# A vision block with routed experts on one core: where the expert numbers are read, when two weight packs are fetched, and where a norm stands

## What is computed

```python
def _L0_ffn_ref(x, router_w, w1, b1, w2, b2, gamma, beta):
    logits = xf @ router_w
    gate_vals, idx = jax.lax.top_k(logits, K)        # K = 2 of 8 experts
    gates = jax.nn.softmax(gate_vals, axis=-1)
    out = jnp.zeros_like(xf)
    for e in range(E):
        h = jax.nn.relu(xf @ w1[e] + b1[e]) @ w2[e] + b2[e]
        y = _layernorm(xf + h, gamma[e], beta[e])
        w = jnp.sum(jnp.where(idx == e, gates, 0.0), axis=-1)
        out = out + w[:, None] * y
    return out.reshape(B, S, D)
...
h = h + _L0_attn_ref(_layernorm(h, axis=-1), ...)
h = h + _L0_ffn_ref(_layernorm(h, axis=-1), ...)
```

## Time and profile before

| | |
|---|---|
| median of 3 runs | 144.37 us (144.24 to 144.65) |
| profiled execution, its own time | 144.59 us |
| its span, first to last instruction | 142.8 us |
| PE busy | 130.9 us (92% of the span) |
| VectorE busy | 104.4 us (73%) |
| ScalarE busy | 72.9 us (51%) |
| POOL busy | 57.3 us (40%) |
| mean granted TensorE clock | 0.940 |

### The profile page before, as it was taken

The page is one execution under the profiler, slowest core; times in us unless marked ns, Lnnn a source line. Parts: engine busy times, 40 slices in busy tenths (PEclk is TensorE's granted clock), DMA queues, the critical chain, the costliest instruction groups (busy, mean ns, idle before and its releaser), DMA issues. The chain is left out here.

```text
span 142.8 us, 3886 instructions
## 1 busy us (share of the span) xinstructions
PE 130.9 (92%) x1210; PEld 114.2 (80%) x1210; DVE 104.4 (73%) x417; ACT 72.9 (51%) x214; POOL 57.3 (40%) x96
## 2 busy tenths in 40 slices
PE   7999899999999999889993899999999999999960
PEld 7944898788759898668930879999999999999950
DVE  1479999979988667778664029887878789988580
ACT  5534315834476531139900006887878977896000
POOL 8900000000000046775778131377677767680010
PEclk9999999999999999999555569999999999999999
DMA  4999399999993019611115477598999751015405
GB/s 117 263 457 418 156 387 414 404 339 274 278 270 113 5 17 333 255 50 56 45 56 101 179 166 221 133 317 277 243 334 311 239 163 41 21 33 167 175 0 149
DMA packets 16423, 28.47 MB, mean 199 GB/s; under 512 B 1793, under 2 KB 9878, under 8 KB 16276
## 3 DMA queue, kind: packets, MB, share of 16 engines
q1 hardware_dynamic: 13700, 25.43, 55.3%
q0 software_dynamic: 1152, 2.07, 4.3%
q10 hardware_dynamic: 1552, 0.73, 2.2%
HBM read 19.55 MB, written 12.09 MB: 222 GB/s over the span
## 5 line engine op out<-in xcount | busy, mean ns | idle before, releaser
L1457 PE MATMUL ps<-w_all,hid 128*128 (+1 forms) x184 | 24.7, 278 | 0.3 <-issue 0.2
L1457 PEld LDWEIGHTS ps<-w_all,hid 128*128 128x128 f32 x184 | 22.4, 192 | 1.0 <-issue 0.8
L503 POOL DMA_INDIRECT back<-kTm,xg x16 | 15.9, 997 | 12.2 <-ACT kTm L693 6.1
L684 ACT ACTIVATE hid<-ps,D 128x128 f32<-128x128 f32 x48 | 13.5, 362 | 13.7 <-PE ps L1438 13.7
L1150 PE MATMUL ps<-zeros 128*128 128x128 f32 x112 | 17.8, 312 | 2.9 <-POOL SQ L490 2.9
L1150 PEld LDWEIGHTS ps<-zeros 128*128 128x128 f32 x112 | 16.1, 222 | 3.9 <-POOL SQ L490 3.4
L471 POOL TENSOR_TENSOR ex<-e_base,dlt 128x5 f32<-128x5 f32 x1 | 1.2, 1207 | 44.8 <-DVE dlt L935 44.8
L464 POOL DMA_INDIRECT rows<-x2k,row_at x16 | 16.1, 1007 | 6.9 <-issue 5.0
L1054 DVE COPY xgT<-ps 128x128 f32<-128x128 f32 x23 | 6.7, 290 | 10.1 <-PE ps L1430 8.4
L1438 PE MATMUL ps<-xgT,D 128*128 128x128 f32 x96 | 12.8, 276 | 0.0
L684 ACT ACTIVATE hid<-ps,last_parts 128x128 f32<-128x128 f32 x44 | 12.4, 364 | 0.0
(11 more groups left out here) (236 smaller groups left out, 278.4 us busy)
## 6 DMA issues: line engine op xcount, KB each, us to landing
rows<-blank SPq DMA_DIRECT2D x8, 589.5 KB, 6.7
D<-pack SPq DMA_DIRECT2D x12, 386.0 KB, 5.2
last_parts<-pack SPq DMA_DIRECT2D x11, 386.0 KB, 4.8
pack<-w1b SPq DMA_DIRECT2D x1, 2064.0 KB, 15.6
w_all<-w SPq DMA_DIRECT2D x1, 2048.0 KB, 12.2
back<-zeros SPq DMA_DIRECT2D x1, 1152.0 KB, 9.0
xg<-rows SPq DMA_DIRECT2D x16, 65.5 KB, 3.0
xT_oT<-patches SPq DMA_DIRECT2D x2, 512.0 KB, 5.9
```

The costliest lines, as they stand in the source:

```text
L503: nc.gpsimd.indirect_dma_start(back, bass.IndirectOffsetOnAxis(ap=xg[j][:, P:P + 1].bitcast(U32), axis=0), z[j], None, bounds_check=P * K ...
L684: nc.scalar.activation(hid[j % 2][:, f, :], ps[:, 2 + 2 * (j % 2) + f // 2, f % 2 * P:(f % 2 + 1) * P], ACT.Relu, bias=packed[j % NW][:, H ...
L1457: last = mm(ps[:, 6 + j % 2, 0:P], hid[j % 2][:, f, :], w2_all[:, bass.ds(expert_j, 1), f, :].rearrange("p a n -> p (a n)"), start=(f == 0 ...
```

## The change

Four edits:

1. PE reads all 18 expert numbers in front of the loop, right behind the matmuls on beta (line 1424) and ahead of the warming matmuls; `second_product` then takes them from a list. PE's wait for `slots_done` moves there too.
2. SP holds the packs of slots 5 and 6 back: it first reads its expert and tile numbers and issues the four local row loads, then these two packs.
3. VectorE's `normalise_group(3)`, the norm of tiles 7 and 8, moves from ahead of `rank_tables(1)` to behind `places(1)`. On PE `rank(1)` moves ahead of `turn_norm2(2)` with it.
4. On ACT `twice(1)`, a copy, moves behind the loading of the table for Exp and the exponential of part 1.

```diff
@@ sync
+            expert_at(0)
-            for j in range(FIXED, FIRST_ROWS):
-                load_pack(j)
             tile_at(FIRST_ROWS - FIXED)
             for j in range(SENT, SLOTS):
                 tile_at(j - FIXED)
             for j in range(SENT, SLOTS):
                 load_rows(sp, j, tile_at(j - FIXED))
+            for j in range(FIXED, FIRST_ROWS):
+                load_pack(j)
             sp.wait_ge(xg_loaded[row_sem(2)], 16)
@@ scalar
-            twice(1)
             nc.scalar.activation(table_scrap[:, 3:4], zeros[:, 0:1], ACT.Exp)
             exp_gates(1)
+            twice(1)
             copy_norm2(2)
@@ vector
             choose(1)
-            normalise_group(3)
             rank_tables(1)
             gates(1)
             places(1)
+            normalise_group(3)
             choose(2)
@@ tensor
             keep_warm(KEEP_WARM[9], 2)
+            rank(1)
             turn_norm2(2)
-            rank(1)
             route(2)
@@ tensor, the loop
-            w2_experts = {}
+            pe.wait_ge(slots_done, 2)
+            w2_experts = list(range(FIXED))
+            for s in range(0, FREE, 4):
+                w2_experts += list(four_values(mybir.EngineType.PE, expert_of, s, EXPERTS - 1))
 
             def second_product(j):
-                if j < FIXED:
-                    expert_j = j
-                else:
-                    if j not in w2_experts:
-                        for i, x in enumerate(four_values(mybir.EngineType.PE, expert_of, j - FIXED, EXPERTS - 1)):
-                            w2_experts[FIXED + (j - FIXED) // 4 * 4 + i] = x
-                    expert_j = w2_experts[j]
+                expert_j = w2_experts[j]
...
             pe.wait_ge(token_cols_set, 1)
             keep_warm(REWARM, 7)
-            pe.wait_ge(slots_done, 2)
```

## The result

The changed kernel takes **147.55 us** (median of 4 runs, 147.34 to 147.98) where the kernel before, beside it on the same chip, takes 144.48 (144.24 to 144.65, 4 runs). The ratio is 1.0217, with a 95% interval of 1.0188 to 1.0246. It is slower by 3.1 us. The profiled execution of it took 147.34 us, with a span of 145.5 and a mean granted clock of 0.928 (0.940 before).

A forecast was written before the change was run, and what follows sets the result against it. PE was taken to bound the end. Late warming +4.9, clock -0.2 and gaps -1.23 make +3.5 us on the profiled 144.59, so 148.1, or 147.8 as median (0.22 lower); own range 146.3 to 148.9, outer ends 145.5 and 149.3.

The forecast's parts named there:

- slots_done: Slot numbers ahead of PE's reads: ready at 76.3, not 73.80, from 1.7 us of later norm and 0.8 of half clock.
- Five reads, 7.8 us: PE's queue ahead of the warming: five reads of expert numbers take 7.8 us together, bounds 6.5 and 8.5.
- The rival in which reads are cheap in front: Ahead of the warming: all five reads fit into the idle 2.88 us, leaving only the saving, 143.3 us; chance 0.07.
- The warming +4.9: Ahead of PE's expert loop: the warming starts when the reads end, at 84.1 and not 79.20, +4.9 us.
- The clock, worth -0.2: During the warming: full clock returns after about 5.0 us, 0.4 less at half clock, -0.2 us; bounds -0.9 and +0.9.
- The gaps, -1.23: In PE's expert loop: array time lost at the first four reads (0.47, 0.21, 0.24, 0.31) goes away, -1.23 us.
- The end is PE's: Last stretch, 128 to 138: PE is busy throughout, so moving its loop's start or a slot moves the end equally.
- The rows down at 80.4, worth nothing: Row dispatch before the loop: rows down at 80.4, not 81.6, a 1.2 us gain alone, counted as nothing behind late warming.
- rival 3: Ahead of the reads: the norm's move is absorbed, slots_done stays at 73.8, reads end at 81.6, 145.5 us; chance 0.12.
- the sum said +3.5: Whole kernel: +4.9 - 0.2 - 1.23 = +3.5 us against the profiled execution's 144.59, that is 148.1.

The follow-up runs named there:

- b1: The kernel before with only the first three of PE's five reads in front of the warming, the last two in the loop; ratio 0.9984.
- b0: The changed kernel as it is, run again on another chip; ratio 1.0212 to the kernel before.
- c3: The changed kernel as it is, run again on a further chip beside its two halves; ratio 1.0164 to the kernel before.
- b2: The kernel before with nine reads of two values in place of five of four, all in the loop; ratio 0.9895.
- c4: The kernel before with nine reads of two values inside the loop and the two packs held back; 149.95 us, ratio 0.9801.
- c2: The changed kernel with PE's reads put back into the loop (norm's move and held-back packs stay); ratio 0.9912 to the kernel before.
- a1: The changed kernel with PE's reads put back into the loop, on another chip; ratio 1.0073 to the kernel before.
- b3: The changed kernel with the ten warming matmuls ahead of the five reads; ratio 1.0372 to the kernel before.

## Why the prediction was right

The time, 147.55, was forecast at 147.8, and the cause that it names, the reads ahead of the warming behind late slot numbers, is what the profile shows. By its own steps:

- **slots_done** at 76.3: it came at 76.22. The norm was 1.56 us late (1.7 said), and the routing matmuls lost about 0.8 to the half clock, as said.
- **Five reads, 7.8 us**: 7.5, from 76.3 to 83.8, with the loads at 0.35 us in the median and the register steps behind them the greater part. The rival in which reads are cheap in front fell with this. By the Trainium skill's floor of 600 ns for a `tensor_load` (DMA: Bandwidth & Descriptors, "Latency and other measured facts") five would be 3.0 us, an estimate; the trace disagrees with both, with 0.35 us for the load and 7.5 for the five reads. b1 showed the condition that the rival hung on: even three reads, 5.2 us, overran the idle time, by 0.5.
- **The warming +4.9**: +4.66 (83.86 for 79.20).
- **The clock, worth -0.2**: this term was mis-sized. The clock returned after 3.2 us and not 5.0, so the passes took 3.99 us, 0.65 less, and the first slot 1.65 and not 1.83. The step counted on one delay for all executions; the bound of -0.9, for a return within 3.6 us, holds it. The 0.16 us of waiting for rows is gone too, and the first transpose starts 0.16 us ahead of the modelled end of the last pass. So the loop started 3.69 us late and not 4.7.
- **The gaps, -1.23**: all four are gone; between the loop's start and the last pick the kernel regains 1.28 us (3.69 to 2.41). The gaps are 1.21 of that; the first slot's 0.18 and 0.12 lost just ahead of the picks nearly cancel.
- **The end is PE's**: this reading was wrong, though it cost little. TensorE is busy to the end, but VectorE's last additions start when the rows are back by DMA and run without a pause to the stores, and the last of them begins 0.4 us after the last pick's end before and 0.7 after. The loads of these rows were issued 2.45 us later (131.57 for 129.12) and took 0.26 us longer, together the 2.7 of the stores. The delay of the loop reached them through its last scatters, so that the sum held. The 0.26 is not the change's: the same stretch took 9.28 us in after and 9.10 and 8.99 in b0 and c3, 9.01 before.
- **The rows down at 80.4, worth nothing**: the row loads began at 79.92, GpSimd used the first rows at 81.88, 2.24 us after the iota, and TensorE came for them at 87.69. Right here, since the reads make the warming late; b2 and c4 show that without the reads in front this part is what lets the loop start on time, which the text ahead did mark (a warming that ends at 82.7 or earlier).
- **The norm's move is absorbed** (rival 3): only without the reads. In the changed kernel the reads start on `slots_done`, so all 2.42 us by which it was late are in the warming's +4.66; counted from the iota, which is itself late by the norm's move, 0.8 to 0.9 us more than with the reads alone.

Profiled execution against profiled execution the change is +2.75 us where the sum said +3.5: 0.24 too much for the reads, 0.63 for the clock (0.45 in the passes, 0.18 in the first slot), 0.32 for the rows' wait and the overlap at the loop's start, against 0.12 too little for the loop's end and 0.3 for the tail. The medians differ by 3.1 us, so the forecast of the time is closer than its sum. That closeness is in part luck: terms of opposite sign cancelled, and the profiled execution was the fastest of the four (147.34 to 147.98).

## What to carry to other kernels

Here the register reads on TensorE's own queue cost mostly by the value, about 0.3 us each beside a load of 0.35 to 0.58 (an estimate from 1.5 us for a read of four and 1.1 for one of two), and they cost the array what no queued work covers. Look first for how long each stretch can hide (here 1.1 us beside queued products, about 5 us of idle time behind `slots_done`), and cut the reads to that length; gathering them all in one place turned five mostly hidden ones into 7.5 us in a row on the path. Parts of one change can have opposite signs, and one that is hidden under another shows its worth only when the other is taken out: the reads were the bad part, and the held-back packs, of no use behind a warming that was late anyway, let the loop of c4 start 1.2 us sooner than that of b2.

## What was not expected of the hardware

- The granted clock returned 3.2 us after the 20 passes began in the changed kernel, 5.4 us in the kernel before and 5.1 us in b2, where the array had by then been idle for 0.4 us. In c2 and a1, one kernel on two chips, it came back before 72 in the one and not in the other, and one VectorE step came 1.1 us sooner for it.
- In b3, 4.64 us of steady passes at 0.50 did not bring the clock back at all: the array then idled 3.64 us and it stayed low until shortly before 98, 4 us into the loop.
- A load of two values took 0.55 us in the median (b2) where one of four took 0.35 (after), and in the changed kernel itself the last load, of two values, took 0.54; the whole read of two was still shorter, 1.1 us to 1.5, by the register steps of two values that it lacks.
- From one profile to the next the same reads differed: three took 5.2 us in b1, with one assertion of 0.64 us, where the first three of the changed kernel took 4.9 (76.3 to 81.2).
- On TensorE's queue the first read of b3 started 0.6 us after the first of 20 passes, 4 us before the last ended: its queue does run ahead of the array there.
